# Layer-0 routed experts: the Gelu products are turned behind the next block's gate and up products, the down products come two blocks later, and GpSimd issues the down loads two blocks behind the others

## The reference, cut to what matters

```python
def _experts_all(x, g, gb, w1, b1, w2, b2):
    y = jax.nn.gelu(jnp.einsum('bsd,edf->bsef', x, g) + gb, approximate=False)
    y = y * (jnp.einsum('bsd,edf->bsef', x, w1) + b1)
    return jnp.einsum('bsef,efd->bsed', y, w2) + b2
aff = jax.nn.sigmoid(jnp.einsum('bsd,de->bse', x, wa))
topk_p, topk_i = jax.lax.top_k(aff, K)
```

## Time and profile before

| | us |
|---|---|
| median of 3 runs | 1599.05 (1598.6 to 1601.68) |
| the profiled execution | 1595.75 |
| its span, first to last instruction | 1594.0 |
| stage of the change, first gate-and-up block to last result | 432.0 to 688.7 |
| mean granted TensorE clock over the span | 0.920 |

### The profile page before, as it was taken

How to read it: one execution, slowest core, us unless ns; L and a number is a source line. 1 busy time by engine, 2 the same in 40 slices (tenths; PEclk the granted TensorE clock), 3 DMA queues, 4 the chain that set the end, 5 groups by cost and what they waited for, 6 DMA issues and landing times. The chain is left out here.

```text
span 1594.0 us, 21478 instructions
## 1 busy us (share of the span) xinstructions
PE 1354.6 (85%) x7253; PEld 1117.2 (70%) x7253; DVE 1075.5 (67%) x1794; ACT 728.8 (46%) x1157; POOL 735.1 (46%) x654
## 2 busy tenths in 40 slices
PE   5999869999699999936999689996788899999960
PEld 5787647766377777726999688985566777777740
DVE  5688757232388888865885556674493688888857
ACT  4121132000188888822555354440422488888850
POOL 1445510000488887634664233431055466666634
PEclk8899979999799999968999789997798799999985
DMA  4000040000456566642110000000513899999958
GB/s 166 1 1 27 27 133 2 1 0 0 173 189 215 174 214 220 226 119 55 53 41 1 34 1 1 27 27 27 195 40 115 317 340 344 346 348 344 344 132 316
DMA packets 81807, 212.67 MB, mean 133 GB/s; under 512 B 20425, under 2 KB 23497, under 8 KB 79291
## 3 DMA queue, kind: packets, MB, share of 16 engines
q1 hardware_dynamic: 50075, 133.14, 22.8%
q0 software_dynamic: 31120, 77.38, 17.2%
q10 hardware_dynamic: 528, 1.05, 0.2%
HBM read 208.75 MB, written 46.79 MB: 160 GB/s over the span
## 5 line engine op out<-in xcount | busy, mean ns | idle before, releaser
L66 PE MATMUL bank<-e_w_hi,e_xt_hi 128*96 128x384 f32 (+1 forms) x444 | 168.8, 380 | 3.4 <-DVE e_w_lo L2563 3.4
L2453 POOL DMA_INDIRECT sums<-e_y,r_target_of x64 | 121.8, 1902 | 88.4 <-DMA sums<-e_y,r_target_of 69.7
L68 PE MATMUL bank<-e_w_hi,e_xt_lo 128*96 128x384 f32 (+1 forms) x444 | 161.3, 363 | 0.0
L67 PE MATMUL bank<-e_w_lo,e_xt_hi 128*96 128x384 f32 (+1 forms) x444 | 160.8, 362 | 0.0
L1064 POOL DMA_INDIRECT e_w_raw<-in_w_gate_up,r_load_of x47 | 53.6, 1141 | 215.4 <-issue 215.4
L1189 DVE TENSOR_TENSOR e_w_lo<-e_w_raw,e_w_hi 128x2048 fp32r<-128x2048 f32 x47 | 107.8, 2293 | 33.7 <-ACT e_w_hi L1148 33.7
L2563 DVE TENSOR_TENSOR e_w_lo<-r_w_early,e_w_hi 128x1536 fp32r<-128x1536 f32 x48 | 84.4, 1758 | 24.3 <-ACT e_w_hi L2527 24.3
L1056 POOL DMA_INDIRECT e_xg<-rows,r_token_of x47 | 93.1, 1980 | 14.3 <-issue 14.3
L231 POOL TENSOR_TENSOR a_read<-a_read_n 128x256 f32<-128x256 f32 x64 | 50.3, 785 | 103.0 <-DVE a_read_n L452 103.0
L1687 POOL TENSOR_TENSOR q_g_lo<-q_gf,a_g 128x512 fp32r<-128x512 f32 x32 | 41.6, 1299 | 112.9 <-ACT a_g L1801 112.9
L1148 ACT ACTIVATE e_w_hi<-e_w_raw 128x2048 fp32r<-128x2048 f32 x47 | 89.7, 1909 | 0.0
(11 more groups left out here) (461 smaller groups left out, 4335.0 us busy)
## 6 DMA issues: line engine op xcount, KB each, us to landing
r_w_early<-in_w_gate_up SPq DMA_DIRECT2D x48, 768.0 KB, 16.0
r_w_early<-in_w_down SPq DMA_DIRECT2D x24, 768.0 KB, 12.9
results<-e_y SPq DMA_DIRECT2D x47, 256.0 KB, 3.7
rows<-resid SPq DMA_DIRECT2D x8, 1024.0 KB, 4.3
r_w_first<-in_w_gate_up SPq DMA_DIRECT2D x8, 768.0 KB, 15.9
e_w_raw<-in_w_down SPq DMA_DIRECT2D x8, 768.0 KB, 13.2
e_w_raw<-in_w_gate_up SPq DMA_DIRECT2D x8, 768.0 KB, 15.5
resid<-in_x SPq DMA_DIRECT2D x4, 1024.0 KB, 11.5
```

What stands on the lines that cost most here:

```text
L66: pe.matmul(out, a_hi, b_hi, start=start, stop=False)
L67: pe.matmul(out, a_hi, b_lo, start=False, stop=False)
L68: return pe.matmul(out, a_lo, b_hi, start=False, stop=stop)
L2453: pool.indirect_dma_start(k.sums[p % 2], bass.IndirectOffsetOnAxis(k.target_of[:, e:e + 1], 0), y[p][:, :], None, compute_op=ALU.add).then ...
```

## The change

TensorE's step g becomes turn(g+1), gate_up(g), turn_hidden(g-1), down(g-2), with one more step at the end. ScalarE and VectorE get a new helper, `pipeline`, that takes each stage with its own distance. ScalarE's step is turned_hi(g+1), weights_hi(g+1), gelu(g), hidden_hi(g-1), down_hi(g-1), results(g-2), where `down_hi` is the split of the down weights that used to be part of `gelu`; VectorE's is turned_lo(g+1), weights_lo(g+1), hidden(g), hidden_lo(g-1), down_lo(g-1). On GpSimd, from block 4 on, the down load issued with rows and gate_up of block g is that of block g-2.

```diff
+def pipeline(eng, n, unroll, *stages):
+
+    def step(g):
+        for stage, ahead in stages:
+            if 0 <= g + ahead < n:
+                stage((g + ahead) // unroll, (g + ahead) % unroll)
+
+    first, last = -max(ahead for _, ahead in stages), -min(ahead for _, ahead in stages)
+    rounds = (n + first - 1) // unroll
+    for g in range(first, 2 * unroll + 1):
+        step(g)
+    with eng.Fori(2, rounds) as i:
+        for q in range(unroll):
+            for stage, ahead in stages:
+                stage(i + (q + 1 + ahead) // unroll, (q + 1 + ahead) % unroll)
+    for g in range(unroll * rounds + 1, n + last):
+        step(g)
...
-                for g in range(U, NG0):
-                    rows(g // U, g % U)
-                    gate_up(g // U, g % U)
-                    down(g // U, g % U)
+                for g in range(U, NG0 + 2):
+                    for stage, item in ((rows, g), (gate_up, g), (down, g - 2)):
+                        if U <= item < NG0:
+                            stage(item // U, item % U)
...
-                for g in range(-1, NG0 + 1):
-                    for stage, item in ((turn, g + 1), (turn_hidden, g - 1), (gate_up, g), (down, g - 1)):
+                for g in range(-1, NG0 + 2):
+                    for stage, item in ((turn, g + 1), (gate_up, g), (turn_hidden, g - 1), (down, g - 2)):
...
-                def gelu(h, p):
+                def down_hi(h, p):
                     g = U * h + p
                     act.wait_ge(s_v[p], 16 * (h + 1))
                     if past(h, p, 2):
                         act.wait_ge(s_dn, g - 1)
                     act.activation(w2_hi[p][:, :], w2_raw[p][:, :], ACT.Copy).then_inc(s_vhi, 1)
+
+                def gelu(h, p):
+                    g = U * h + p
                     act.wait_ge(s_gu, g + 1)
...
-                three_stages(act, NG0, turned_hi, gelu, results, between=hidden_hi, prepare=weights_hi, unroll=U)
+                pipeline(act, NG0, U, (turned_hi, 1), (weights_hi, 1), (gelu, 0), (hidden_hi, -1), (down_hi, -1), (results, -2))
...
-                    vec.wait_ge(s_vhi, g + 1)
+
+                def down_lo(h, p):
+                    vec.wait_ge(s_vhi, U * h + p + 1)
                     vec.tensor_tensor(w2_lo[p][:, :], w2_raw[p][:, :], w2_hi[p][:, :], ALU.subtract).then_inc(s_vlo, 1)
 
-                three_stages(vec, NG0, turned_lo, hidden, nothing, between=hidden_lo, prepare=weights_lo, unroll=U)
+                pipeline(vec, NG0, U, (turned_lo, 1), (weights_lo, 1), (hidden, 0), (hidden_lo, -1), (down_lo, -1))
```

## The result

| | before | changed |
|---|---|---|
| median of the runs, us | 1598.82 (4 runs) | 1618.49 (4 runs) |
| the profiled execution, us | 1595.75 | 1617.08 |
| its span, us | 1594.0 | 1615.3 |
| first gate_up of block 1 | 437.74 | 436.99 |
| first gate_up of block 46 | 680.40 | 699.77 |

The change makes the kernel 1.2% slower: ratio 1.0119, 95% interval 1.0106 to 1.0132. Nearly all of it lies in this stage: its last result comes 21.4 us later, the profiled execution is 21.3 us longer.

The account below looks back on a forecast made before the run. TensorE bounds it now, with a 0.39 us wait a step; afterwards GpSimd's caught transfers make loads late. Block 1 at 437.15, seven steps of 5.15, 38 of 5.90, with the end +19.0: 1614.8, median 1618, range 1590 to 1625.

Parts of the forecast that it names:

- the 3.3 us that I added: Whole kernel: the profiled execution lies 3.3 us below the median of the runs, taking 1614.8 to 1618.
- TensorE's own step: TensorE, each step after the change: work of 5.13 us plus 0.02 for loop ends, 5.15, the 0.39 wait gone.
- VectorE's 4.09 us: VectorE, long subtraction's start to short one's end: 4.09 us, formerly 3.76, leaving a gap of 1.06 instead of 1.62.
- Two transfers a step, and an edge at 1.15: GpSimd at TensorE's pace: two transfers a step where a block needs three; the third needs a gap of 1.15 us.
- Late loads from block 9: Weight loads: the lead of 5 to 8 us lasts through blocks 1 to 8 at 5.15, then loads are late.
- 5.90 us a block after that: The 38 steps behind block 8, with loads late: 5.90 us each, bounded below by 5.24 and above by 5.83 or 6.03.
- the blend of 5.83 and 6.03: Late-load steps: two parts 5.83 (four transfers, then two) to one part 6.03 (five, then two), giving 5.90 a block.
- The ends: Stage start and end: block 1 at 437.15 instead of 437.74, -0.6; bias matmul of block 46 to last result +2.05.
- the first: Rival, chance 0.17: GpSimd not caught by a third transfer or need not keep pace; every step 5.15, 1589.6 us.
- The second: Rival, chance 0.10: steps settle at 5.24, each a little stretched so the third transfer fits; 1593.7 us.
- Any 0.1 us a step would cost 4 us and save 20: TensorE or ScalarE: any uncounted 0.1 us a step would make the forecast wrong, costing 4 us and saving 20.
- What I said of the Trainium skill's rule: GpSimd's indirect transfers read indices from SBUF and are caught by two-input subtractions, against the page's inference that descriptor generation is not stalled.

Follow-up runs that it names:

- experiment 1: The changed kernel with one swap on VectorE: low half of the down weights before the low hidden part; 1585.88 us, ratio 0.9924 to the kernel before.
- experiment 2: The changed kernel with down loads issued by SyncE as plain transfers, one for every block, always of expert p's weights; 1590.33 us, one run.
- experiment 6: The changed kernel with GpSimd's down loads as plain transfers that read no index, one for every block, always expert p's weights; 1589.02 us, one run.
- experiment 5: The changed kernel with VectorE's two subtractions back to back: long, short, product, low hidden part; 1593.37 us, one run.

## Why the prediction was right

The forecast was 1618 us, the measured median 1618.49. The mechanism was right in the main; that the numbers agree to half a microsecond is luck in part. On the profiled execution the forecast was 1614.8 and the measurement 1617.08, 2.3 us more; and the 3.3 us that I added from there to the median were 1.4 (1618.49 - 1617.08). Point by point:

- **TensorE's own step**, 5.15: measured 5.10 (experiment 1, 45 steps, all but the first between 5.02 and 5.19). Right within 1%.
- **VectorE's 4.09 us** from the start of the long to the end of the short subtraction: 525.08 to 529.17 is 4.09. The gap came out at 0.93 to 1.09, for 1.06.
- **Two transfers a step, and an edge at 1.15**: shown. In the changed kernel a third transfer is caught after gaps up to 1.09 and gets through in gaps of 1.19 and more; of the four gaps of 1.12 and 1.13, one was too short and three were not. Two such places, VectorE and GpSimd:

```profile
535.34 2.29 DVE L1211 TENSOR_TENSOR e_w_lo<-e_w_raw,e_w_hi 128x2048 fp32r<-128x2048 f32 x1 [0.52 <-ACT e_w_hi L1167]
...
583.79 2.36 DVE L1211 TENSOR_TENSOR e_w_lo<-e_w_raw,e_w_hi 128x2048 fp32r<-128x2048 f32 x1 [0.53 <-ACT e_w_hi L1167]
```
```profile
535.39 3.11 POOL L1091 DMA_INDIRECT e_w_raw<-in_w_down,r_load_of  x1 [0.30 <-issue]
...
583.83 0.99 POOL L1091 DMA_INDIRECT e_w_raw<-in_w_down,r_load_of  x1 [0.30 <-issue]
```

  A start 0.05 us into the long subtraction is caught, one 0.04 us into it is not (there VectorE waits instead, 2.36 for 2.29). I had put the edge at the subtraction's start; it lies 0.04 behind it.
- **Late loads from block 9**: the steps grow from block 10.
- **5.90 us a block after that**: the 38 steps behind block 8 took 702.63 - 475.34 = 227.3 us, 5.98 each. The term was right in kind and 3 us short in sum (38 x 0.08). The picture behind it, steps of 5.15 and of 6 to 8 alternating, was not: late loads gather, one long step of up to 12.4 us lets GpSimd issue up to seven transfers, and then several short steps use that lead up. And 9.6 us of these 227.3 are products at the low clock, for which the sum has no term. Without them it would be (227.3 - 9.6) / 38 = 5.73 a block, an estimate that leaves all else as it was. So the blend of 5.83 and 6.03 stood near the value partly by luck.
- **The ends**: -0.6 was -0.75 at block 1; 4.88 to 6.9 at the end was 709.51 - 702.63 = 6.88.
- **The rivals**: the first, 1589.6 if GpSimd keeps up, is what experiments 1, 2 and 6 give (1585.9, 1590.3, 1589.0), so its sum was right and only its condition was not met. The second, steps of 5.24 that hold the third transfer by a hair, are the steps that two more transposes give, 5.26; but there TensorE's own work sets them (5.07 + 0.19), not a stretching by GpSimd. In the changed kernel it does not settle there: a caught transfer costs GpSimd half a step at once, and nothing lengthens VectorE's step until a load is late.
- **"Any 0.1 us a step would cost 4 us and save 20"**: wrong as it stands. One tenth made the stage 3.7 us longer and saved nothing; two tenths were needed, and three gave the 22 us.
- **What I said of the Trainium skill's rule**: SBUF — State Buffer, "Who interferes with whom", holds that a two-input subtraction contends with a GpSimd instruction that reads SBUF, and not with one that only writes. Experiment 6 fits both halves, if the plain transfers read nothing from SBUF, which no run here shows: the indirect transfers are caught, the plain ones (0.58 us inside a subtraction) are not. The page's inference that descriptor generation is not stalled held here for plain transfers only.

Settled only in part: why single steps reach 12 us. Waits for rows and weights and the slow products behind them add up to it; why the late loads fall together just there would take the order of real and skipped loads, which was not varied. The stage starts late in some runs, by up to 6 us (first bias at 436.2 to 442.0), which is why it is compared by itself. In experiments 5 and 6 and with one more transpose the delay lies ahead of the stage: its first transposes start at 428.6 to 428.8, against 424.1 before and changed, and the granted clock from 350 to 400 us was 0.93, against 0.97. The late start of experiment 2 (440.36) was not traced.

## What to carry to other kernels

Before taking a wait out of a pipeline, list what else runs once per step on every engine, GpSimd's descriptor work above all, and ask at which step time it stops fitting; here the new order took 0.33 us from a gap that the shorter step was already shrinking, and a miss of some 0.1 us turned a gain of 12 us into a loss of 20. When the transfers of GpSimd show durations of two sizes (0.99 and over 1.4 us), set their starts against VectorE's instructions with two SBUF inputs. Then move the starts apart, not the work: one swap on VectorE gives 1585.9 us, 0.8% under the kernel before and the best of all versions here.

## What the runs showed of the hardware

- An indirect transfer that GpSimd starts inside a VectorE subtraction with two SBUF inputs ends 0.82 to 0.91 us after that subtraction, wherever within it it starts (from about its last 0.05 us on it takes 0.96 to 1.00 us, as when free). One that starts up to 0.04 us behind the subtraction's start still gets through in 0.96 to 0.99 us, and the subtraction then takes 2.32 to 2.37 us instead of 2.29; at 0.05 us it is caught.
- A VectorE instruction with one input in PSUM (`bank`) does not catch it: in experiment 5, 39 indirect transfers start inside one with no subtraction running (one at 524.77, 0.12 us into the product), and take 0.96 to 1.00 us.
- Between two such subtractions that follow each other with no pause (0.02 to 0.08 us of overlap in the profile of experiment 5) a waiting transfer gets through: all 44 that began in the long one ended 0.85 to 0.87 us after it.
- A plain transfer issued by GpSimd takes 0.58 us and is not held by a subtraction (ten cases in experiment 6).
- Behind two waits of 1.88 and 2.69 us TensorE's clock was at its lower level for some 7 us, and the 12 gate-and-up products took 5.14 us instead of 2.85.
